# Where 128 small clips of squared norms are computed: on VectorE behind the sum, or on GpSimd ahead of its power

## The reference

```python
for l in range(DEPTH):                       # DEPTH = 2
    h = shift_token(x)                       # half of the columns come from the row before
    q, k, v = split(h @ wqkv[l])             # 8 heads of 64 columns
    q = l2norm(q) * q_scale[l]
    k = l2norm(k) * k_scale[l]
    q, k = rotary_xpos(q, k)
    x = x + local_attention(q, k, v) @ wo[l]
    h = shift_token(x)
    h = layernorm(h) * ln_g[l] + ln_b[l]
    a, g = split(h @ w1[l] + b1[l])
    x = x + (a * gelu(g)) @ w2[l] + b2[l]

def l2norm(t):
    return t / jnp.clip(jnp.linalg.norm(t, axis=-1, keepdims=True), 1e-12)
```

## Time and profile before

| | us |
|---|---|
| three runs: median (lowest to highest) | 3000.75 (2998.53 to 3004.02) |
| the profiled execution's own time | 3003.69 |
| its span, first to last instruction | 3001.9 |
| TensorE busy | 2734.4 |
| VectorE busy | 2489.0 |
| ScalarE busy | 1793.8 |
| GpSimd busy | 1343.1 |
| TensorE's mean granted clock | 0.986 of full |

### The profile page before, as it was taken

One profiled execution on the slowest core, in us unless ns is written; L12 is line 12 of the kernel. 1 busy time (PEld: TensorE's weight loads), 2 busy tenths in 40 slices (PEclk: granted clock), 3 DMA queues, 4 the chain that ended last, 5 costly groups with the idle time before them and its releaser, 6 DMA issues.

```text
span 3001.9 us, 63211 instructions
## 1 busy us (share of the span) xinstructions
PE 2734.4 (91%) x21452; PEld 1918.9 (64%) x21452; DVE 2489.0 (83%) x7195; ACT 1793.8 (60%) x4181; POOL 1343.1 (45%) x949
## 2 busy tenths in 40 slices
PE   2399998999899998899989999899998999899997
PEld 2167675676666676666756767567765667666675
DVE  3489888888889887898878988889887988889895
ACT  2147673577646776376754767457764677637674
POOL 1145443545335454455534544344543545435552
PEclk9799999999999999999999999999999999999999
DMA  5100001000000000000010000100000000000000
GB/s 157 34 2 6 7 5 36 3 6 4 22 21 5 5 7 24 15 5 5 8 30 9 6 4 8 36 3 5 5 22 20 5 5 7 24 15 5 5 8 18
DMA packets 57996, 46.29 MB, mean 15 GB/s; under 512 B 18466, under 2 KB 54988, under 8 KB 57556
## 3 DMA queue, kind: packets, MB, share of 16 engines
q1 hardware_dynamic: 53520, 35.14, 4.2%
q10 hardware_dynamic: 4164, 7.12, 0.7%
HBM read 25.42 MB, written 8.44 MB: 11 GB/s over the span
## 4 chain that ended last, share of the span: by engine, by line
PE 64%; DVE 12%; ACT 6%; POOL 5%; issue 5%; DMA 4%; DVEq 0%; ACTq 0%; POOLq 0%
PE ps L134 11%; PE ps L135 11%; PE ps L136 11%; PE ps L400 8%; PE ps L426 7%; PE ps L411 5%; PE ps L335 4%; DMA XS<-xu 4%; PE ps L386 2%; PE ps L354 2%; ACT ar_b L569 2%; PE ps L294 2%; DVE ar_b L796 2%; POOL small L907 1%; DVE ar_b L780 1%
## 5 line engine op out<-in xcount | busy, mean ns | idle before, releaser
L907 POOL TENSOR_TENSOR small<-small,neg_half 128x16 f32<-128x16 f32 x128 | 406.2, 3174 | 416.7 <-DVE small L743 414.9
L569 ACT ACTIVATE ar_b<-ar_b,small 128x256 f32<-128x256 f32 (+1 forms) x1024 | 492.9, 484 | 103.6 <-DVE small L780 100.9
L780 DVE CUSTOM_DVE_ANT_0 ar_b<-ps,mask_t,small 128x256 f32<-128x256 f32 (+1 forms) x1024 | 419.5, 462 | 28.3 <-PE ps L400 25.1
L911 POOL TENSOR_TENSOR ar_c<-ar_c 128x1024 f32<-128x1024 f32 x128 | 301.9, 2358 | 229.7 <-DVE ar_c L769 229.0
L796 DVE TENSOR_SCALAR ar_b<-ar_b,rsw 128x256 f32<-128x256 f32 (+1 forms) x1024 | 302.9, 359 | 9.2 <-DVE rsw L789 0.2
L242 POOL TENSOR_SCALAR stats<-stats 128x2 f32<-128x2 f32 x128 | 29.9, 234 | 596.5 <-DVE stats L828 259.0
L134 PE MATMUL ps<-wqkv_hi,ht_hi 128*128 128x512 f16 x768 | 292.0, 380 | 0.0
L135 PE MATMUL ps<-wqkv_lo,ht_hi 128*128 128x512 f16 x768 | 291.1, 379 | 0.0
L136 PE MATMUL ps<-wqkv_hi,ht_lo 128*128 128x512 f16 x768 | 291.1, 379 | 0.0
L400 PE MATMUL ps<-ar_a 64*128 64x128 f32 x3840 | 271.4, 285 | 15.6 <-ACT ar_a L559 15.6
L411 PE MATMUL ps<-id_f,ar_b 128*128 128x128 f32 x1920 | 269.9, 276 | 17.0 <-DVE ar_b L796 16.5
(11 more groups left out here) (170 smaller groups left out, 6669.2 us busy)
## 6 DMA issues: line engine op xcount, KB each, us to landing
xu<-in_L_attn_x_dram SPq DMA_DIRECT2D x32, 256.0 KB, 2.9
out_dram<-xu SPq DMA_DIRECT2D x64, 128.0 KB, 2.8
XS<-xu SPq DMA_DIRECT2D x128, 63.5 KB
ar_a<-in_L_ffn_wqkv_dram ACTq DMA_DIRECT2D x1, 3072.0 KB, 16.9
modb<-mod_rows SPq DMA_DIRECT2D x8, 384.0 KB, 5.5
XS<-xu SPq DMA_DIRECT2D x112, 0.5 KB
ar_a<-in_L_wmod_dram SPq DMA_DIRECT2D x1, 1536.0 KB, 7.6
xu<-in_L_ffn_w_dram SPq DMA_DIRECT2D x1, 1364.0 KB, 9.3
```

The costliest lines, as they stand in the source:

```text
L569: last = act.activation(pw, pw, ACT.Exp, bias=mnw[:, n % 2, h:h + 1], scale=-1.0, accum_out=smw[:, n % 2, h:h + 1])
L780: last = dve.tensor_tensor_reduce(out=PW[:, f, q, i, c:2 * P], in0=ps[:, bk, i * 256 + c:(i + 1) * 256], in1=mask_t[:, c:2 * P], scale=rin ...
L907: pool.tensor_tensor(rinv[:, n % 4, :], ssm[:, n % 2, :], neg_half[:, 0:16], ALU.pow).then_inc(s_rinv, 1)
L911: pool.tensor_tensor(M1[:, n % 2, :], M1[:, n % 2, :], M2, ALU.add).then_inc(s_add, 1)
```

## The change

The clip moves from the VectorE piece `ss` to the GpSimd piece `pw`. VectorE's sum of squares now also has the wait for the power of two tiles before, which the clip had. GpSimd waits for the sum, clips, waits for the clip's end, and computes the power. Slots, table and all other pieces stay. In the changed file VectorE's lines behind `ss` have numbers smaller by two (L761 is L759, and so on), and GpSimd's L907 keeps its number.

```diff
@@ -735,12 +735,10 @@
                     elif k == "ss":
                         n, = ids
                         dve.wait_ge(s_sq, at("sq", n))
+                        if n >= 2:
+                            dve.wait_ge(s_rinv, at("pw", n - 2))
                         dve.tensor_reduce(ss[:, n % 2, :], SQ.rearrange("p (h d) -> p h d", d=DH), AX,
                                           ALU.add).then_inc(s_ss, 1)
-                        dve.wait_ge(s_ss, at(*piece))
-                        if n >= 2:
-                            dve.wait_ge(s_rinv, at("pw", n - 2))
-                        dve.tensor_scalar(ssm[:, n % 2, :], ss[:, n % 2, :], 1e-24, None, ALU.max).then_inc(s_rm, 1)
@@ -903,7 +901,9 @@
                     elif k == "pw":
                         n, = ids
-                        pool.wait_ge(s_rm, at("ss", n))
+                        pool.wait_ge(s_ss, at("ss", n))
+                        pool.tensor_scalar(ssm[:, n % 2, :], ss[:, n % 2, :], 1e-24, None, ALU.max).then_inc(s_rm, 1)
+                        pool.wait_ge(s_rm, at(*piece))
                         pool.tensor_tensor(rinv[:, n % 4, :], ssm[:, n % 2, :], neg_half[:, 0:16], ALU.pow).then_inc(s_rinv, 1)
```

## The result

The changed kernel took 3015.3 us in the median of four runs (3012.84 to 3017.79), the kernel before 3001.99 in four runs of the same session (2998.53 to 3004.02). The ratio is 1.0047, 95% interval 1.0032 to 1.0062. So it is slower by 13.3 us, outside the forecast range (2998.5 to 3010.0) and four times the forecast loss of 3.1. The profiled execution took 3015.2 us, span 3013.5, against a span of 3001.9 before.

A forecast was written before the change was run, and what follows sets the result against it. The prediction took TensorE's wait for GpSimd's product at each batch's first tile as the bound. Tile 0's 2.2 us plus tile 1's 0.9, nothing elsewhere, made +3.1 us on 3000.75: 3003.9 us, range 2998.5 to 3010.0.

The forecast's parts named there:

- What bounds the kernel: TensorE 91% busy, VectorE 83%; the clip counts where TensorE waits for GpSimd's product at each batch's first tile.
- Tile 0: First window tile of a batch: power ends at T+4.49, not T+4.22 (T: sum of squares' end); 2.2 us in all.
- Tile 1: Second window tile: GpSimd's row runs on without pause, so 0.11 us of new TensorE waiting a batch, 0.9 us in all.
- The whole 0.33: Clip's cost on GpSimd per tile: 0.24 us for the instruction plus 0.09 us waiting for its own end.
- The cover: Slack at tile 1 between GpSimd's product and TensorE's transposes, said to absorb 0.22 us of the delay.
- VectorE's busy time: Across the kernel, predicted to fall by about 36 us as 128 clips leave VectorE.
- Tile 7: VectorE's copy comes 0.79 us earlier, but TensorE's own L411 must finish; gain counted 0 (0 to 0.14 a batch).
- Tiles 4 and 5: Tile 4's power ends 0.40 us later but is covered, cost 0; tile 5's shift is 0.01 us.
- A: Rival, chance 0.20: tile 0's power also waits at the port for the second L769; 8.5 us slower, 3009.2.
- B: Rival, chance 0.05: tile 0's power holds the port to its end, delaying the second L769; 8.1 us slower, 3008.9.
- C: Rival, chance 0.08: VectorE's time at tiles 7 and 14 reaches TensorE; faster, 2986.8 us, or 2995.3 for half.
- D: Rival, chance 0.09: at tile 0 the power ends where it did and tile 1's cover holds; no change, 3000.8 us.

The follow-up runs named there:

- E14: Changed kernel with 4 to 12 matmuls, results overwritten, in each of TensorE's seven long waits of a batch; 3010.32 us, ratio to before 1.0028.
- E5: Changed kernel with tile 1's clip moved between the root's addition and its power on GpSimd, all instructions kept; 3012.42 us, ratio to before 1.0038.
- E17: Changed kernel with tile 1's clip between the root's addition and its power, and the seven long waits filled with matmuls; 3001.89 us, ratio to before 1.0006.
- E7: Kernel before with one more clip on VectorE at tile 0 of each batch; 3011.38 us, ratio to before 1.0036.
- E9: E8 with eight matmuls, results overwritten, filling TensorE's wait at tile 0; 3011.83 us, ratio to before 1.0033.
- E2: Changed kernel with the clip back on VectorE at tile 1 alone; 3013.56 us, ratio to before 1.0045.
- E8: Kernel before with two more clips on VectorE at tile 0 of each batch; 3012.21 us, ratio to before 1.0034.
- E10: Changed kernel with eight matmuls, results overwritten, filling TensorE's wait at tile 0; 3012.95 us, ratio to before 1.0036.
- E18: Changed kernel with tile 1's clip on VectorE and the seven long waits filled with matmuls; 3003.69 us, ratio to before 1.0010.

## Why the prediction was wrong

Slower had a chance of 0.29, and the forecast sum of 3.1 us was a quarter of the loss.

- **What bounds the kernel: right.** The loss is made at the head of the GpSimd row, at tiles 0 and 1. No half-clock stretch and no wait of the other tiles is needed to explain it (E14).
- **Tile 0: right.** +0.27 forecast, +0.27 to 0.29 in seven of eight batches (0.38 in the first); clip 1.16 us, power issued at T+1.33 and ended at T+4.51.
- **Tile 1: this is the term that failed.** "The whole 0.33 goes on top of tile 0's shift ... 0.11 is new TensorE waiting: 8 x 0.11 = 0.9 us (0 to 0.3 a batch)". It was 0.81 at tile 1 and 0.29 behind it, 8.8 us in all (9.3 with the waits filled), and by itself most of the difference between forecast and result. The cover was read too small: it is 0.42 (8.54 us that the product came later, less 7.31 that tile 0's transposes did, less 0.81), where I had 0.22. I had read it at the weight load, which in the fourth batch before stood 0.22 ahead of the first matmul (1279.65, 1279.87) and now comes with it (both 1287.99). The 0.33 was too small: 1.22. I had walked through the port at tiles 0, 4 and 5 instruction by instruction and left it out at tile 1, where VectorE's L723, which has two SBUF inputs as well, is released by the same end of L244 as GpSimd's next instruction. Before, GpSimd won that tie by 0.06 us. A clip put in front of the power loses it, and then the power loses its turn to L767. E5 and E17 show it: with all the same instructions in another order 0.82 of the 1.17 us goes, 0.60 of it port waits. The engines do not meet through semaphores alone, as the description of the chip at the start has it; this port is where they meet besides.
- **What a late product does to VectorE: not seen.** L794 behind L917, +0.29 at tile 2 and +0.11 at tile 13, was counted as nothing.
- **VectorE's busy time** fell by 25.6 us and not 36. GpSimd's clips were as described: 0.25 us in the median, 1.16 at tiles 0, 5 and 13.
- **Tile 7: too low**, -0.21 and not 0 (0 to 0.14): 1.7 us of gain.
- **Tiles 4 and 5: right.** Tile 4's power ended at the sum's end + 3.98 (forecast 3.96), and cost nothing; tile 5 cost 0.04.
- **The rivals.** A and B did not come: the power took 3.18 at tile 0 (not over 3.5), the pair of L767 1.31 (not over 2). C's gains were but tile 7's, and D, that nothing changes, is out with the ratio's interval. A's time (3009.2) came nearest to the result, for the wrong reason: a second port stop there was, but at tile 1.
- **A wait's price.** Each 0.1 us of TensorE wait was priced at 0.1. In this kernel that holds only while the clock and the order at the port stay: E7 paid 10.2 us for 1.6. For the changed kernel it made no difference in the end, since it has as many half-clock stretches as before in the attention stages (8) and 2 behind tile 0, some 1 us; but it is why no repair of tile 1 alone helped. Why the attention stage takes up the stretches that tile 0 is freed of (E9) stays open.

## What to carry to other kernels

Where an instruction is added in front of another on an engine that shares a port, ask for each place what is released by the same semaphore on the other engine, and who of the two was ahead, and by how much: a lead of 0.06 us decided over most of the 0.8 us at tile 1. Follow the port at every tile that has little cover, not only at the one that is on the chain. And before a wait of TensorE is priced at its length, look in the granted clock for half-speed stretches behind waits of nearly that length: here 0.2 us more in each batch cost 10.2 us in place of 1.6, and a repair gave little until the clock was held.

## What the runs showed of the hardware

- A wait of TensorE of 1.78 us at tile 0 was followed by no stretch at half clock in eight batches; waits of 2.0 to 2.2 us were, in 2 (changed kernel), 2 (E7), 4 (E2), 5 (E5) and 5 (E8) of eight. Each made the way from tile 0 to tile 1 some 1.62 us longer, and hid whatever wait stood at tile 1. A stretch in the attention stage cost 0.4 to 0.9 us.
- Filling the seven long waits of a batch with matmuls that nobody needs kept the clock at full from the first batch to the last: 0.991 in the mean instead of 0.986, and 5 us for the kernel before. Filling tile 0's wait alone took away the stretches behind it, and no time that is clear of the noise (E9, E10).
- What GpSimd holds depends on the instruction. A power on 128x16 (2.9 to 3.2 us) let a pair of L767 run inside it in their bare 1.31; the sum on 128x1024 in E7's fifth batch held VectorE's L703: issued behind the sum's start, it took 2.15 us instead of 0.43 and ended 0.28 us behind the sum.
- GpSimd's max on 128x16 takes 0.25 us alone. In E5, between two instructions of the root, it took 0.33 and the row as a whole only 0.28 more, since it filled the root's wait for its own end.
- GpSimd's gap between L917 and L242 grew from -0.03 to +0.08 us in the changed kernel, though neither instruction nor its waits were changed. It is 0.08 in every run in which tile 0's clip is on GpSimd (E2, E5, E10, E14, E17, E18) and -0.03 in every other; why stays open.
